# Splitting a routed block's load, turning two blocks at once, and moving one inverse deviation from GpSimd to ScalarE and VectorE

## What is computed

```python
h = h + _L1_ffn_ref(_layernorm(h, axis=-1), Wr, br, W1, b1, W2, b2)

def _L1_ffn_ref(x, Wr, br, W1, b1, W2, b2):
    logits = xf @ Wr + br
    topk_logits, topk_idx = jax.lax.top_k(logits, 2)
    gates = jax.nn.softmax(topk_logits, axis=1)
    for e in range(64):
        h = jax.nn.relu(xf @ W1[e] + b1[e])
        y = h @ W2[e] + b2[e]
        out = out + combine[:, e:e + 1] * y
```

## Time and profile before

| | us |
|---|---|
| median of 3 runs | 2447.14 |
| lowest and highest | 2443.28 and 2456.15 |
| the profiled execution's own time | 2461.87 |
| its span, first to last instruction | 2460.1 |
| routing: first to last indirect send (L1488) | 1735.4 to 2031.2 |
| experts: first to last indirect send (L1503) | 2048.2 to 2432.3 |

### The profile page before, as it was taken

One profiled execution on the slowest core, in us unless ns is written; L12 is line 12 of the kernel. 1 busy time (PEld: TensorE's weight loads), 2 busy tenths in 40 slices (PEclk: granted clock), 3 DMA queues, 4 the chain that ended last, 5 costly groups with the idle time before them and its releaser, 6 DMA issues.

```text
span 2460.1 us, 55471 instructions
## 1 busy us (share of the span) xinstructions
PE 1800.5 (73%) x17723; PEld 1396.3 (57%) x17723; DVE 1667.0 (68%) x5137; ACT 1118.7 (45%) x3614; POOL 1067.9 (43%) x846
## 2 busy tenths in 40 slices
PE   5788897999999999999999456775333326656650
PEld 2366776777777777777777245554221215555550
DVE  0057773478888888888887589995888863333332
ACT  2477772244444444444443369884221115444430
POOL 0046660134443433443433322221677774555553
PEclk9889996699999999999998579878555555555555
DMA  9910000000000000000000000002300012111104
GB/s 284 274 60 0 0 0 1 1 2 2 2 0 0 0 0 0 0 0 0 0 0 1 1 1 1 1 0 114 92 22 21 21 66 58 43 40 40 41 27 165
DMA packets 79641, 84.93 MB, mean 35 GB/s; under 512 B 53792, under 2 KB 68256, under 8 KB 78240
## 3 DMA queue, kind: packets, MB, share of 16 engines
q1 hardware_dynamic: 66064, 66.50, 9.7%
q0 software_dynamic: 13312, 13.85, 1.7%
q10 hardware_dynamic: 144, 3.15, 0.3%
HBM read 55.78 MB, written 27.69 MB: 34 GB/s over the span
## 4 chain that ended last, share of the span: by engine, by line
PE 30%; DVE 23%; issue 16%; POOL 13%; another core or an unknown queue 8%; DMA 5%; ACT 3%; DVEq 1%; POOLq 0%; SPq 0%; ACTq 0%
POOL routed_rows L1488 8%; PE PS L698 5%; DMA arena<-in_x_dram 4%; PE PS L665 4%; PE PS L732 4%; PE PS L713 3%; POOL rstd L1389 2%; DVE XR L1644 2%; DVE XR L1844 1%; DVE arena L2026 1%; DVE arena L2040 1%; DVE XR L1640 1%; PE PS L747 1%; PE PS L772 1%
## 5 line engine op out<-in xcount | busy, mean ns | idle before, releaser
L1503 POOL DMA_INDIRECT expert_rows<-arena x224 | 219.4, 980 | 181.7 <-DMA expert_rows<-arena 111.7
L1112 ACT ACTIVATE arena<-PS 128x384 f32<-128x384 f32 (+2 forms) x376 | 162.8, 451 | 220.6 <-PE PS L665 69.9
L1640 DVE TENSOR_REDUCE XR<-PS 128x2 f32<-128x192 f32 (+2 forms) x768 | 173.9, 280 | 111.8 <-PE PS L698 111.8
L1488 POOL DMA_INDIRECT routed_rows<-XR,SLu x192 | 209.1, 1089 | 81.0 <-issue 74.2
L1359 ACT ACTIVATE XR<-arena 128x257 f32 x448 | 158.1, 408 | 181.0 <-DVE arena L2046 103.5
L698 PE MATMUL PS<-arena 32*128 32x96 f32 (+2 forms) x3072 | 235.8, 286 | 0.0
L698 PEld LDWEIGHTS PS<-arena 32*128 32x128 f32 x3072 | 200.0, 193 | 20.8
L2026 DVE TENSOR_TENSOR arena<-PS,XR 128x512 f32<-128x512 f32 x56 | 38.7, 692 | 240.0 <-remote 200.7
L1434 POOL TENSOR_TENSOR arena<-arena,mhalf 96x16 f32<-96x16 f32 x32 | 93.3, 2916 | 241.5 <-DVE arena L1686 241.5
L1148 ACT ACTIVATE XR<-PS 128x256 f32<-128x256 f32 x512 | 167.3, 380 | 67.5 <-PE PS L713 67.3
L1112 ACT ACTIVATE XR<-PS 128x384 f32<-128x384 f32 (+1 forms) x160 | 83.5, 523 | 225.6 <-PE PS L732 171.2
(11 more groups left out here) (309 smaller groups left out, 4765.6 us busy)
## 6 DMA issues: line engine op xcount, KB each, us to landing
arena<-in_x_dram SPq DMA_DIRECT2D x32, 784.0 KB, 10.6
arena<-in_t_experts_dram SPq DMA_DIRECT2D x8, 1028.0 KB, 12.3
routed_rows<-zt SPq DMA_DIRECT2D x14, 528.0 KB, 6.1
arena<-routed_rows SPq DMA_DIRECT2D x56, 132.0 KB
expert_rows<-arena POOLq DMA_INDIRECT x224
WP<-in_t_pack_dram SPq DMA_DIRECT2D x1, 3428.5 KB, 21.0
mixed_rows<-Hb SPq DMA_DIRECT2D x4, 768.0 KB
routed_rows<-XR,SLu POOLq DMA_INDIRECT x192
```

Of the source, the lines that this page charges most:

```text
L1112: return act.activation(dst, src, ACT.Identity, **kw)
L1488: pool.indirect_dma_start(XD, bass.IndirectOffsetOnAxis(SLu[:, u, k, b:b + 1], 0), XG[:, u, b, k, :], None).then_inc(scat[u], 16)
L1503: pool.indirect_dma_start(YD, bass.IndirectOffsetOnAxis(yi[:, u % 4, k:k + 1], 0), yb[:, u % 4, k, :], None).then_inc(e_st[u % 2], 16)
L1640: dve.tensor_reduce(negmax[:, p, j, :], PS[:, S_:S_ + 2, S_AT[j]:S_AT[j] + QB * (j + 1)], AX_X, ALU.max, negate=True).then_inc(b_max, 1)
```

## The change

In the experts, rows and labels of a group go to two tiles by two DMAs (64 floats and 2 floats of each row), so that two blocks lie side by side in one tile and PE turns a pair of them with one full transpose, two a group. The order in which the blocks' weights lie in the ring follows. In the routing, POOL's power goes away; ACT takes a square root as the last stage of its step, DVE a reciprocal in front of the multiplication, and `d_norm` goes ahead of `d_center` in DVE's order.

```diff
+def place(i):
+    return i // 2 % 2 * KB + i // 4 * 2 + i % 2
...
-        xb = te("xb", [P, RING, KB, ROW])
+        xb = te("xb", [P, RING, KB, D])
+        xm = te("xm", [P, RING, KB, ROW - D])
...
-                wait(sp, e_in[u % 4], (g - u % 4) * 4)
+                wait(sp, e_in[u % 4], (g - u % 4) * 8)
...
-                sp.dma_start(xb[:, u, :, :], XD[ds(g * (EB * SLOT), EB * SLOT)].rearrange("(k p) d -> p k d", p=P)
-                             ).then_inc(e_in[u % 4], 16)
+                rows = XD[ds(g * (EB * SLOT), EB * SLOT)].rearrange("(k p) d -> p k d", p=P)
+                sp.dma_start(xb[:, u, :, :], rows[:, :, 0:D]).then_inc(e_in[u % 4], 16)
+                sp.dma_start(xm[:, u, :, :], rows[:, :, D:ROW]).then_inc(e_in[u % 4], 16)
...
-                pe.wait_ge(e_in[u % 4], (g - u % 4) * 4 + 16)
+                pe.wait_ge(e_in[u % 4], (g - u % 4) * 8 + 32)
...
-                for k in range(KB):
-                    for h in range(2):
-                        r = slice(h * SLOT, (h + 1) * SLOT)
-                        mm = pe.matmul(PS[r, u % 2, k * SLOT:(k + 1) * SLOT], xb[r, u, k, 0:D], ident[r, r], start=True, stop=True)
+                for m in range(KB // 2):
+                    mm = pe.transpose(PS[:, u % 2, m * P:(m + 1) * P], xb[:, u, 2 * m:2 * m + 2, :].rearrange("p k d -> p (k d)"), ident[:, :])
...
-            grouped(act, NR, (0, d_squares), (1, d_features), (1, d_logitsS), (2, d_gate_exp), (2, d_keep))
+            def d_root(g, u):
+                act.wait_ge(ln_var, LD + g + 1)
+                wait(act, ln_xn, LD + g - 1)
+                act.activation(dst[:, u, 3, :], dst[:, u, 2, :], ACT.Sqrt).then_inc(ln_rstd, 1)
+
+            grouped(act, NR, (0, d_squares), (1, d_features), (1, d_logitsS), (2, d_gate_exp), (2, d_keep), (0, d_root))
...
-            def d_power(g, u):
-                pool.wait_ge(ln_var, LD + g + 1)
-                wait(pool, ln_xn, LD + g - 1)
-                pool.tensor_tensor(dst[:, u, 3, :], dst[:, u, 2, :], mhalf[0:NTOK, 0:GD], ALU.pow).then_inc(ln_rstd, 1)
...
-            grouped(pool, NR, (2, d_scatter(0, 2)), (0, d_power), (1, d_label), (2, d_scatter(2, NV)))
+            grouped(pool, NR, (2, d_scatter(0, 2)), (1, d_label), (2, d_scatter(2, NV)))
...
                 dve.wait_ge(ln_rstd, LD + g + 1)
                 wait(dve, ln_xT, LD + g - 1)
+                link = Link(dve, ln_chain, g, 3, 2)
+                link.base += 2 * NG + NG * 5 + 2 * NR
+                link(dve.reciprocal(dst[:, u, 3, :], dst[:, u, 3, :]))
...
-            grouped(dve, NR, (0, d_center), (1, d_norm), (2, d_places), (0, d_var), (1, d_best))
+            grouped(dve, NR, (1, d_norm), (0, d_center), (2, d_places), (0, d_var), (1, d_best))
...
-                dve.tensor_copy(yi[:, u % 4, :], xb.bitcast(U32)[:, u, :, D])
+                dve.tensor_copy(yi[:, u % 4, :], xm.bitcast(U32)[:, u, :, 0])
```

More of the change, by code:

```diff
@@ L991, in e_hidden @@
                         r = slice(h * D, (h + 1) * D)
-                        mm = pe.matmul(PS[:, 2 + 4 * h + u % 2, k * SLOT:(k + 1) * SLOT], wx[r, (u + 2) % WRING, 2 * k + h, 0:NHX],
+                        mm = pe.matmul(PS[:, 2 + 4 * h + u % 2, k * SLOT:(k + 1) * SLOT], wx[r, (u + 2) % WRING, h * KB + k, 0:NHX],
                                        xT[r, u % 2, k * SLOT:(k + 1) * SLOT], start=True, stop=True)
@@ L1000, in e_output @@
                     for h in range(2):
-                        at = (h * KB + k) * SLOT
+                        i = place(2 * k + h)
+                        at = i * SLOT
                         mm = pe.matmul(PS[h * SLOT:(h + 1) * SLOT, 4 + u % 2, k * D:(k + 1) * D], hT[:, u % 2, at:at + SLOT],
-                                       wx[:, (u + 2) % WRING, 2 * k + h, NHX:NHX + D], start=True, stop=True)
+                                       wx[:, (u + 2) % WRING, i, NHX:NHX + D], start=True, stop=True)
                 mm.then_inc(e_down, 1)
@@ L1358, in pick_weights @@
                     e = (four >> (6 * (k % PACK))) & (NX - 1)
-                    a = act.activation(wx[:, (u + 2) % WRING, k, :], wall[:, ds(e, 1), :].rearrange("p o w -> p (o w)"), ACT.Identity)
+                    a = act.activation(wx[:, (u + 2) % WRING, place(k), :], wall[:, ds(e, 1), :].rearrange("p o w -> p (o w)"), ACT.Identity)
                 a.then_inc(e_w, 1)
@@ L1921, in d_center @@
             def d_center(g, u):
-                link = Link(dve, ln_chain, g, 2)
+                link = Link(dve, ln_chain, g, 3)
                 link.base += 2 * NG + NG * 5 + 2 * NR
@@ L2027, in e_relu @@
                                        PS[:, 2 + u % 2:8:4, 0:KB * SLOT].rearrange("p h (k r) -> p h k r", r=SLOT),
-                                       wx[:, (u + 2) % WRING, :, BIAS].rearrange("p (k h) -> p h k", h=2).unsqueeze(3)
+                                       wx[:, (u + 2) % WRING, :, BIAS].rearrange("p (h k) -> p h k", h=2).unsqueeze(3)
                                        .broadcast_to([P, 2, KB, SLOT]), ALU.add))
@@ L2039, in e_out @@
                     r = slice(h * SLOT, (h + 1) * SLOT)
-                    add = dve.tensor_tensor(yb[r, u % 4, :, :], PS[r, 4 + u % 2, 0:KB * D].rearrange("p (k d) -> p k d", k=KB),
-                                            wx[r, (u + 2) % WRING, h::2, NHX + D:NHX + 2 * D], ALU.add)
+                    add = dve.tensor_tensor(yb[r, u % 4, :, :].rearrange("p (m q) d -> p m q d", q=2),
+                                            PS[r, 4 + u % 2, 0:KB * D].rearrange("p (m q d) -> p m q d", q=2, d=D),
+                                            wx[r, (u + 2) % WRING, h::2, NHX + D:NHX + 2 * D].rearrange("p (q m) d -> p m q d", q=2), ALU.add)
                     if h == 0:
@@ L2046, in e_out @@
                 dve.tensor_tensor(yb[:, u % 4, :, :], yb[:, u % 4, :, :],
-                                  xb[:, u, :, D + 1:D + 2].broadcast_to([P, KB, D]), ALU.mult).then_inc(e_y, 1)
+                                  xm[:, u, :, 1:2].broadcast_to([P, KB, D]), ALU.mult).then_inc(e_y, 1)
             grouped(dve, NBLK // EB, (1, e_relu), (2, e_out), unroll=RING)
```

## The result

| | before | after |
|---|---|---|
| median, us | 2448.63 (6 runs) | 2433.09 (6 runs) |
| lowest and highest | 2443.28, 2456.15 | 2424.33, 2436.77 |
| the profiled execution's own time | 2461.87 | 2424.5 |
| its span | 2460.1 | 2422.7 |

The changed kernel takes 0.9928 of the time before, 95% interval 0.9901 to 0.9956: 15.5 us less, faster by more than the 0.5% that can be told from no change. 2432 us were forecast.

A forecast was written before the change was run, and what follows sets the result against it. Routing was held bound by a loop through POOL's power and DVE, the experts by POOL's four sends and landing. Gains of 18.0 us less 3.0 lost gave 15.0, so 2447.14 - 15.0 = 2432 us, range 2420 to 2452.

The forecast's parts named there:

- The round: Routing: without POOL's power the period falls from 19.04 to 17.5 us, set by DVE; thirteen intervals gain 20.0 us.
- The last two intervals: End of the routing: the last two rounds, paced by POOL, gain about 1 us net.
- The start: First routing rounds: nothing covers load, root and reciprocal; 3.0 us lost once, bounds 1.5 and 4.5.
- Table loads: ACT in the routing: two loads a round, 1.30 us each, stay hidden; slack 1.7 us at the exponential.
- Transposes: PE in the experts: at most 1.1 us a group saved, but POOL does not wait for PE; 0 us.
- Split load: Experts: two DMAs a group disturb POOL's fourth send by 0.05 us a group; 3 us lost in all.
- A: Experts: the split load collides with POOL's last send, 36 us lost, 18 gained, 2465 us; chance 0.10.
- C: Routing: ACT becomes late, the exponential misses DVE by a microsecond a round, 2446 us; chance 0.12.
- D: Experts: PE sets the pace, so shorter turns save 0.6 us a group, 33 us, giving 2399 us; chance 0.05.
- B: Routing: POOL's sends stretch beside DVE's work, the round stays at 18.5, gain about nothing, 2446 us; chance 0.13.
- the forecast's own range: Whole kernel: 2424 us (round at 17.1, no disturbance) to 2440 (round at 17.9); the forecast has chance 0.60.
- the chance of 0.5 for faster: Whole kernel: faster by more than 0.5%, below 2434.9 us; 0.45 from the forecast, 0.05 from D.

The follow-up runs named there:

- chip Y: Chip of one follow-up group; the changed kernel, run again unaltered there, took 0.9925 of the kernel before.
- Z: Chip of another follow-up group; the changed kernel, run again unaltered there, took 0.9984 of the kernel before.
- experts alone: Changed kernel with the routing of the kernel before (power on POOL, old DVE order), against the kernel before: ratio 0.9991.
- no table switch: Changed kernel with a square in place of ACT's square root, so no table load in the rounds; 0.9924 of the kernel before.
- X: Chip of a third follow-up group; kernel before with only the routing edits 1.0080, changed kernel with DVE's old order 1.0107 of the kernel before.

## Why the prediction was right, and where it was not

The forecast itself came true, 2432 for 2433, faster, and so did the mechanism: the loop through POOL's power is gone and DVE sets the round. That the number was met within a microsecond is in part luck, since the terms were too small by some 7 us and the first medians show 15.5 of the 22 us that the last layer gained. The terms below take the changed kernel where completions are in time; the kernel before has only profiles with late ones (see above).

- **The round.** 17.5 us forecast, 17.29 measured as the mean, 17.35 in the steady rounds. The 13 intervals gain 22.0 us, 20.0 were forecast. The wait itself was sized rightly, 1.72 and 1.92 us in turn, 1.82 on average (27.5 / 14 is more, since the last one is 3.45), and so was the reciprocal, 0.23 with its link. What was left out stands in the rows: without the wait, the next instruction starts before the recorded end of the one ahead of it. From L1927 to the next instruction it is 2.54 us on average over ten rounds before, and 0.62 after (1849.87 - 1849.22 = 0.65 in the round above): 1.92 less and not 1.82. Everything else that DVE does in a round, line by line, is the same within 0.04 us.

```profile
1834.51 0.76 DVE L1927 TENSOR_TENSOR XR<-Hb,arena 96x512 f32<-96x512 f32 x1
1836.98 0.69 DVE L1937 TENSOR_TENSOR XR<-XR,arena 96x512 f32<-96x512 f32 x1 [1.72 <-POOL arena L1473]
```

- **The last two intervals.** 35.3 to 33.0 us, 2.3 gained for 1.0.
- **The start.** 2.2 us lost for 3.0. The second squares came 2.3 us later and not 2.6 (1699.40, 3.83 us behind the end of L1938, where the earlier trace rows have 1.54): half of the difference is that the load began with the end of the squares and not behind v + eps; the rest is that reciprocal and multiply took 0.85 us to the next instruction and not 0.95, and the centring 1.63 to the squares and not 1.7. The 0.4 us put on for what stands behind them did not show.
- **Table loads.** Hidden, with the slack that was worked out, 1.64 us for 1.7. The other price that stood beside it was that of the Trainium skill, "ScalarE: Activation LUTs", section "What ACT_TABLE_LOAD costs" (the prediction names the section behind it), 2.66 us a switch; the trace has 1.28 and the next activation 0.01 later, for either table, so the trace does not agree.
- **Transposes.** 0, as forecast.
- **Split load.** 0 and not 3 us lost. The step that failed is the 0.05 us a group for a disturbance: the last packet of both loads was through at 2188.68, 0.75 us ahead of the fourth send. The prediction gave the second load up to the time of the first, about 1 us; its pieces took 9 ns each against 20, and all but 0.2 us of them ran beside the first load.

In sum 22 to 23 us in the last layer (754.0 to 731.0), not 15. The median on chip Y moved by 20.1 us, the first one by 15.5, on Z by 6.3; the stages ahead of the layer scatter by more than this difference, since the layer began between 1690.2 and 1706.1 us in the profiles of this study.

**The rivals.** A fell with experts alone, C with no table switch, D with rows of 55 landings before and after. B had the right outcome for Z, for the wrong reason: there the gain is within the noise, but not since sends stretch (mean 1050 ns on Y, 1060 on Z, 1089 before). The upper end of the forecast's own range, 2440 with a round at 17.9, does not follow from the prediction's terms, which give 2437; nothing hangs on it. What no rival foresaw is that a kernel can lose its gain to completions that arrive late. On X the two kernels with root and reciprocal that ran there were slower than before; the changed kernel did not run on X, so what it would lose there is open. So the chance of 0.5 for faster was for one chip; on Z the answer would have been no difference.

**What stays open** is what makes the completions late. What the runs show of it: those of engines come in the stretches in which POOL's indirect sends run, from DVE, PE and ACT alike; on another chip the same program has none in the routing and few in the experts (14 of 334 on Y between 2060 and 2290 us, 102 of 345 on Z). The Trainium skill, "SBUF — State Buffer", section "Who interferes with whom", has VectorE and GpSimd share one pair of ports and nobody else; a lock between these two would not hold PE back, and one program ran with and without late completions, so no run here speaks for it as the cause. A rival that no run tests is the recording itself: the trace of the changed kernel holds 19560 updates of semaphores on Y and 14378 on Z, and every run of this study has its span and granted clock on record, so none can be taken as free of it.

## What to carry to other kernels

Two engines that are tied hide each other in a chain of waits: lay both beside each other in order of time, take the slower one's busy time without its waits as the new period. Here that gave the round within 0.2 us. Ask of every wait on a landing whether the buffer behind it is really needed: here it cost five times what the whole change brought. And measure a change of under 1% on more than one chip before it is believed; a part that was run alone on another chip had the wrong sign.

## What was not expected of the hardware

- One program, 2425.5 us on one chip and 2447.5 on another, while the kernel before had 2445.6 and 2453.8: the changed kernel's difference is 13.8 us the larger, and its last layer differs by 12.8, most of it in rounds with completions of DVE, PE and ACT that reach their semaphore 1 to 3 us late (4.5 in one case) while indirect sends run.
- A profile shows that state by DVE waiting on "remote" behind finished work, and by a missing time to landing of the indirect sends. It is plainest in the updates of the semaphores: 0 of 743 completions without one in time on Y, 308 of 735 on Z.
- A table load can begin ahead of its activation's own wait (1841.12 for a root at 1843.44), so an alternation of exponential and root cost only what lay on the path: 1.1 us once, in 30 loads, on chip Y.
- 512 pieces of 8 B behind 512 of 256 B took 9 ns each against 20 and cost nothing that could be measured.
- An engine's instruction that need not wait starts before the recorded end of the one ahead (0.07 us at 1849.87), so a wait that goes away brings a little more than its own length.
